# Routing each sequence inside the output projection, into one region per expert, with the modulation weights loaded early and the clearing moved into the attention

## The reference

```
x1  = x0 + gate * (attention(...) @ Wo)
h   = layernorm(x1) * scale + shift
lg  = router(rmsnorm(h))              # [2048 tokens, 8 experts]
top2, weights = top 2 of lg, softmax over the two
xs  = rows of h sorted by expert      # 4096 rows, ragged groups
y   = gelu(xs @ Wg[e]) * (xs @ Wu[e]) @ Wd[e]
x2  = x1 + gate * combine(y, weights)
mod1 = silu(c1) @ L1_wmod             # [4, 3072], six parts of 512, used in layer 1
```

## Time and profile before

| | us |
|---|---|
| median of 3 executions | 2810.01 |
| lowest, highest | 2806.75, 2813.84 |
| the profiled execution, its own time | 2821.85 |
| span of that execution in the trace | 2820.1 |
| mean granted TensorE clock, share of full | 0.934 |
| busy over the span: PE, DVE, ACT, POOL | 2440.6, 1751.6, 1275.8, 1083.1 |

### The profile page before, as it was taken

The page is one execution under the profiler, slowest core; times in us unless marked ns, Lnnn a source line. Parts: engine busy times, 40 slices in busy tenths (PEclk is TensorE's granted clock), DMA queues, the critical chain, the costliest instruction groups (busy, mean ns, idle before and its releaser), DMA issues. The chain is left out here.

```text
span 2820.1 us, 34326 instructions
## 1 busy us (share of the span) xinstructions
PE 2440.6 (87%) x10156; PEld 1660.9 (59%) x10156; DVE 1751.6 (62%) x2565; ACT 1275.8 (45%) x2546; POOL 1083.1 (38%) x1090
## 2 busy tenths in 40 slices
PE   7999959999999986966999994769898757699889
PEld 5778825555555544845888883535445216588767
DVE  4330239999999994644555553679999977211133
ACT  3223038999999982324555552732323113211121
POOL 0102035666666654542000002278898973111110
PEclk9999979999999997967999997889999988899989
DMA  5253343434444427757766765544444435100022
GB/s 176 84 170 129 97 107 106 128 107 124 112 119 117 113 61 226 252 194 256 233 227 227 233 209 160 172 151 153 161 166 156 176 118 173 53 23 22 19 93 67
DMA packets 269652, 399.91 MB, mean 142 GB/s; under 512 B 33392, under 2 KB 116352, under 8 KB 269536
## 3 DMA queue, kind: packets, MB, share of 16 engines
q1 hardware_dynamic: 234848, 347.64, 39.0%
q10 hardware_dynamic: 28704, 33.08, 3.4%
q0 software_dynamic: 5984, 17.73, 1.9%
HBM read 304.09 MB, written 94.31 MB: 141 GB/s over the span
## 5 line engine op out<-in xcount | busy, mean ns | idle before, releaser
L1020 ACT ACTIVATE attn_probs<-attn_ps_score,attn_nmax 128x512 f32<-128x512 f32 x512 | 342.8, 674 | 2.6 <-DVE attn_nmax L1094 2.6
L2480 PE MATMUL scan_ps_o<-scan_qs,scan_sel 128*128 128x512 f32 x512 | 265.3, 635 | 84.3 <-DVE scan_qs L2424 81.7
L2442 DVE TENSOR_TENSOR_SCAN scan_st<-scan_ps_dec,scan_kv 128x512 f32<-128x512 f32 x256 | 305.4, 1207 | 9.9 <-POOL scan_kv L2394 9.8
L928 PE MATMUL attn_ps_score<-attn_KK,attn_X 64*128 64x512 f32 x512 | 215.0, 466 | 20.6 <-ACT attn_probs L1020 20.2
L2480 PEld LDWEIGHTS scan_ps_o<-scan_qs,scan_sel 128*128 128x128 f32 x512 | 88.9, 194 | 232.2 <-DVE scan_qs L2424 153.9
L1108 DVE SCALAR_TENSOR_TENSOR attn_mixed<-attn_probs,attn_cf,attn_mixed 128x512 f32<-128x512 f32 x256 | 193.5, 756 | 9.1
L1083 DVE TENSOR_REDUCE attn_raw<-attn_ps_score 128x2 f32<-128x1024 f32 x128 | 156.4, 1222 | 42.4 <-PE attn_ps_score L928 41.1
L928 PE MATMUL attn_ps_score<-attn_KL,attn_X 64*128 64x512 f32 x512 | 172.9, 422 | 0.0
L85 POOL MEMSET head_ident<- 128x128 f32 x1 | 0.2, 204 | 439.6 <-POOLq L2828 439.6
L2394 POOL TENSOR_TENSOR scan_kv<-scan_vb,gla_gk 128x512 f32<-128x512 f32 x128 | 160.7, 1277 | 12.2 <-DMA scan_vb<-gv 5.4
L928 PE MATMUL attn_ps_score<-attn_KK,attn_Y 64*128 64x512 f32 x512 | 160.1, 397 | 1.3 <-POOL attn_Y L822 1.3
(11 more groups left out here) (438 smaller groups left out, 6803.8 us busy)
## 6 DMA issues: line engine op xcount, KB each, us to landing
scan_vb<-gv SPq DMA_DIRECT2D x256, 256.0 KB
moe_raw<-in_L_ffn_gating SPq DMA_DIRECT2D x92, 512.0 KB
attn_spread<-rows SPq DMA_DIRECT2D x64, 384.0 KB
moe_raw<-in_L_ffn_linear SPq DMA_DIRECT2D x46, 512.0 KB, 5.4
rows_x<-out_zeros SPq DMA_DIRECT2D x23, 512.0 KB, 8.4
moe_xb<-rows_x SPq DMA_DIRECT2D x23, 512.0 KB, 6.1
rows_y<-moe_y ACTq DMA_DIRECT2D x23, 512.0 KB, 6.5
sg<-proj_tile SPq DMA_DIRECT2D x32, 256.0 KB, 2.0
```

The lines of the kernel that those rows point to most:

```text
L928: last = nc.tensor.matmul(ps_score[n][:, j, :], weights, y[p][half, :], start=(r == 0), stop=(r == len(terms) - 1))
L1020: nc.scalar.activation(probs[b][:, at_j, :], ps_score[n][:, j, :], ACT.Exp, bias=nmax[b][:, at_j:at_j + 1], accum_out=Z[b][:, at_j:at_j + ...
L2442: V.tensor_tensor_scan(st[r][:, :], ps_dec[n % 2][:, :], kv[r][:, :], 0.0, ALU.mult, ALU.add).then_inc(st_ready, 1)
L2480: nc.tensor.matmul(ps_o[w][:, :], sel[:, P - GPH - GPH * d:2 * P - GPH - GPH * d], qs[i % RING][:, :], start=(d == 0), stop=(d == HALF - 1 ...
```

## The change

- `rows_x` becomes 8 regions of 2048 rows, one per expert. A token's row in its expert's region needs only the counts of the tokens before it, so each sequence is ranked (`choice`), counted (`count`) and placed (`places`) by itself inside the projection. The logits move from behind a sequence's fourth tile to behind its third, for the sequence before.
- POOL scatters tiles 0 to 11 within the projection, from tile 10 on, and tiles 12 to 15 at the head of the expert mixture. That stage keeps the table of experts and makes a table of each block's first row, which SP reads before it loads a block's rows. Block 0 always belongs to expert 0 and begins at row 0, so neither its weights nor its rows wait for a table.
- The clearing (now 33.5 MB, 32 transfers of 1 MB) is issued in the attention, one behind each unit's `inputs`.
- The six parts of the modulation weights are loaded in the projection; parts 2 to 5 go into buffers that the projection has finished with. Parts 0 and 1 are multiplied behind its last tile and come back to SBUF with eight small transfers in the expert mixture; parts 2 to 5 are multiplied at that stage's start, and POOL bounds the two gates.

```diff
+        zeros = m.sb("zeros", [P, D])
...
+                sp.dma_start(at(fill, u).rearrange("o p t d -> p (o t) d"),
+                             zeros[:, :].unsqueeze(1).to_broadcast([P, E * B * T // (U * P), D])).then_inc(zeroed, 16)
...
+            nc.gpsimd.memset(zeros[:, :], 0.0).then_inc(const_ready, 1)
...
+        late = s["late"] if h is not None else None
+        raw_w = [late[0][:, i, :] if h is not None else m.sb(f"raw_w{i}", [P, D])[:, :] for i in range(RAWS)]
...
-        FILL_FROM = 2
+        SCATTER_BEHIND = 2 * TT + 2
+        MOD_WITH = {3: 2, 6: 0, 9: 1, 13: 3, 14: 4, 15: 5}
...
-                if cleared is not None:
-                    fill = cleared.rearrange("(n p t) d -> n p (t d)", p=P, t=2)
-                    many = fill.shape[0]
-                    if n == FILL_FROM:
-                        sp.wait_ge(zeros_ready, 1)
-                    for k in range((n - FILL_FROM) * many // (NT - FILL_FROM) if n >= FILL_FROM else 0,
-                                   (n + 1 - FILL_FROM) * many // (NT - FILL_FROM) if n >= FILL_FROM else 0):
-                        sp.dma_start(fill[k], zeros[:, :]).then_inc(zeroed, 16)
-            if cleared is not None:
-                sp.wait_ge(zeroed, 16 * many)
...
+                if h is not None and n in MOD_WITH:
+                    k = MOD_WITH[n]
+                    if k == 2:
+                        sp.wait_ge(wlo_ready, KC)
+                    if k == 3:
+                        sp.wait_ge(stored[0], 16 * B // 2)
+                        sp.wait_ge(hn_ready, B - 1)
+                    if k == 4:
+                        sp.wait_ge(tr_done, DC * (B - 1))
+                        sp.wait_ge(scaled, TT * (B - 1))
+                    if k == 5:
+                        sp.wait_ge(olo_ready, NT)
+                    dst = s["mod_x"][:, k, :, :] if k < 2 else late[k - 2][:, :, :]
+                    sp.dma_start(dst, wmod[:, :, k * D:(k + 1) * D]).then_inc(mod_w_in[k], 16)
...
+            def scatter(n):
+                pool.wait_ge(rows_ready, n // TT + 1)
+                pool.wait_ge(shifted, n + 1)
+                scatter_rows(nc, s, n)
...
+                if h is not None:
+                    if n == 1:
+                        route_constants()
+                    if n % TT == 1 and n > TT:
+                        scale(n // TT - 1)
+                    if n >= SCATTER_BEHIND:
+                        scatter(n - SCATTER_BEHIND)
+                for n in range(NT - SCATTER_BEHIND, NT - 2 * TT):
+                    scatter(n)
                 scale(B - 1)
+                for n in range(NT - 2 * TT, NT - TT):
+                    scatter(n)
...
+            def modulation(k):
+
+                pe.wait_ge(mod_w_in[k], 16)
+                pe.wait_ge(gated, NT - 2 + k)
+                for c in range(DC):
+                    last = nc.tensor.matmul(bank[(NT + k) % BANKS][0:B, :], s["sT"][:, 1, c, :], s["mod_x"][:, k, c, :],
+                                            start=(c == 0), stop=(c == DC - 1))
+                last.then_inc(mod_done, 1)
+
+            def count(b):
+
+                if b == 0:
+                    pe.wait_ge(route_const, N_ROUTE)
+                pe.wait_ge(chosen_ready, b + 1)
+                if b == B - 1:
+                    pe.wait_ge(placed, b)
+                flat = s["chosen"][:, TT * b:TT * (b + 1), :].rearrange("p n e -> p (n e)")
+                for k, x in enumerate((earlier, ones)):
+                    last = nc.tensor.matmul(ps_logit[:, (1 + k) * TT * E:(2 + k) * TT * E], x[:, :], flat, start=True, stop=True)
+                last.then_inc(count_done, 1)
...
-                if h is not None and n % TT == TT - 1 and n > TT:
+                if h is not None and n % TT == 2 and n > TT:
                     logits(n // TT - 1)
+                if h is not None and n % TT == 1 and n >= 2 * TT:
+                    count(n // TT - 2)
+            if h is not None:
+                for k in two:
+                    modulation(k)
             turn(B - 1)
             if h is not None:
+                count(B - 2)
                 logits(B - 1)
+                count(B - 1)
...
+                if h is not None and b and t == TT - 1:
+                    router(b - 1)
                 if h is not None and b >= 2 and t == 1:
-                    router(b - 2)
                     squares(b - 2)
             root(B - 1)
             store(B - 1)
+            if h is not None:
+                for k in two:
+                    modulation(k)
+                squares(B - 2)
             take(B - 1)
             if h is not None:
-                for b in (B - 2, B - 1):
-                    router(b)
-                    squares(b)
+                router(B - 1)
+                squares(B - 1)
+                act.wait_ge(mod_stored, 32)
...
+            def choice(b):
...
+                rc.step(V.tensor_tensor(beats[:, :, :, :], pj, pi, ALU.is_gt))
+                rc.link(V.tensor_tensor(ties[:, :, :, :], pj, pi, ALU.is_equal))
+                rc.link(V.tensor_tensor(ties[:, :, :, :], ties[:, :, :, :], below[:, :, :, :], ALU.mult))
+                rc.link(V.tensor_tensor(beats[:, :, :, :], beats[:, :, :, :], ties[:, :, :, :], ALU.add))
+                rc.link(V.tensor_reduce(rank[:, :, :], beats[:, :, :, :], AX.X, ALU.add))
+                V.tensor_scalar(s["chosen"][:, tiles, :], rank[:, :, :], 2.0, None, ALU.is_lt).then_inc(chosen_ready, 1)
+                rc.step(V.tensor_scalar(s["first_e"][:, tiles, :], rank[:, :, :], 0.0, None, ALU.is_equal))
+                rc.link(V.tensor_scalar(s["second_e"][:, tiles, :], rank[:, :, :], 1.0, None, ALU.is_equal))
+
+            def places(b):
+
+                tiles = slice(TT * b, TT * (b + 1))
+                counts = lambda k: ps_logit[:, (1 + k) * TT * E:(2 + k) * TT * E].rearrange("p (n e) -> p n e", e=E)
+                base = s["base"]
+                dve.wait_ge(count_done, b + 1)
+                for t in range(TT):
+                    n = TT * b + t
+                    rc.link(V.tensor_tensor(base[:, n + 1, :], base[:, n, :], counts(1)[:, t, :], ALU.add))
+                V.tensor_tensor(place[:, :, :], base[:, tiles, :], counts(0), ALU.add).then_inc(placed, 1)
+                dve.wait_ge(placed, b + 1)
+                for c, one in enumerate((s["first_e"], s["second_e"])):
+                    rc.link(V.tensor_tensor(pick[:, :, :], place[:, :, :], one[:, tiles, :], ALU.mult))
+                    rc.link(V.tensor_reduce(s["row"][:, c, tiles], pick[:, :, :], AX.X, ALU.add))
+                V.tensor_copy(row_x[:, :, tiles], s["row"][:, :, tiles]).then_inc(rows_ready, 1)
...
+                    if h is not None and b:
+                        choice(b - 1)
                 if t == 2 and b:
                     after(b - 1)
+                if h is not None and t == 1 and b >= 2:
+                    places(b - 2)
+            if h is not None:
+                places(B - 2)
             after(B - 1)
+            if h is not None:
+                choice(B - 1)
+                places(B - 1)
...
-            for k in range(6):
-                sp.dma_start(mod_w[k][:, :, :], wmod[:, :, k * D:(k + 1) * D]).then_inc(mod_in[k], 16)
-            sp.wait_ge(experts_ready, 1)
-            sp.wait_ge(mod_done, 6)
...
-                sp.dma_start(xb[n % 2][:, :, :], xg[n]).then_inc(xb_in[n % 2], 16)
+                r = nc.sync.value_load(start_of[0:1, n:n + 1], min_val=0, max_val=LAST_START) if n else 0
+                sp.dma_start(xb[n % 2][:, :, :], s["rows_x"][bass.ds(r, BLK), :].rearrange("(t p) d -> p t d", p=P)
+                             ).then_inc(xb_in[n % 2], 16)
 
             load_weights(0)
             sp.wait_ge(scattered, 16 * 2 * NT)
             load_rows(0)
+            sp.wait_ge(experts_ready, 2)
             load_rows(1)
             for n in range(NBLK):
                 if n + 1 < NBLK:
                     load_weights(n + 1)
                 if n + 2 < NBLK:
                     load_rows(n + 2)
+                if n == 1:
+                    for q in two:
+                        for c in range(DC):
+                            at = q * D + c * P
+                            sp.dma_start(s["modT1"][:, q, c, :], s["mod"][1, :, at:at + P].rearrange("b p -> p b"),
+                                         allow_slow_non_contiguous=True).then_inc(modT_in, 16)
+            sp.wait_ge(modT_in, 16 * 2 * DC)
...
+            for n in range(NT - TT, NT):
+                scatter_rows(nc, s, n)
...
+            for j, k in enumerate(GATES):
+                line = mod_row[k]
+                pool.wait_ge(mod_taken, k - 1)
+                ch.link(nc.gpsimd.tensor_scalar(sgn, line, 0.0, 2.0, ALU.is_ge, ALU.mult))
...
+            for k in range(2, 6):
+                pe.wait_ge(s["mod_w_in"][k], 16)
+                for c in range(DC):
```

(4 more changed lines are left out.)

278 lines of the change are left out of this document (135 added, 143 removed).

## The result

The kernel after takes 2788.4 us, median of five runs (2783.7 to 2798.5), beside 2808.9 for the kernel before in the same runs (2803.2 to 2813.8): ratio 0.9937, interval 0.9909 to 0.9964, 20.5 us less. Forecast were 2769.0, 40.8 less. Two further sets of the same kernel, measured later, gave 2786.9 (0.9902, 0.987 to 0.9935) and 2780.6 (0.9892, 0.9873 to 0.9911). So the kernel is faster by 20 to 32 us where 41 were forecast; the sign was right and the size too large, by 9 us in the last set and by half the forecast in the first.

A forecast was written before the change was run, and what follows sets the result against it. DVE fills the attention and PE the mixture; between them engines work alone, with a 74.3 us head. Head -54.0, projection +7.0 and tail +6.2 sum to -40.8: from the 2810.0 median to 2769, range 2757 to 2787.

The forecast's parts named there:

- the 8.7 us behind the last scatter issue: Head: landing, loading block 0, turning and splitting it after the last scatter issue, taken as 8.7 us as before.
- the clearing at cost 0: Attention: the clearing moved there is hidden, cost 0, with bounds 0 and 5.1 us a unit.
- POOL in the tail, "to 22": Tail: POOL scales to 12.0 us after the last tile's end, then scatters tiles 8 to 11 (10.1), to 22.
- rival 3: Head: the weights or a later link set gate(0) at 30 rather than 20, giving 2779; chance 0.10.
- `inputs` has been issued when the fill comes: Attention: `inputs` is issued before the fill, and what stands behind is needed most of a unit (21 us) later.
- DVE stays at 97%: Attention: sign of being right, DVE's busy share stays at 97% in the after profile.
- Rival 4: Attention: clearing holds up mask rows or values on an in-order queue; at 5.1 us a unit, 2932; chance 0.04.
- Rival 1: Tail: POOL and DVE in each other's way, issues at 1.9 + 0.3, stage ends 4 to 10 later, 2776; chance 0.20.
- The row that spoke against the page, an issue of 1.89: Profile before: a scatter issue took 1.89 beside DVE's subtractions; the page says tensor_tensor does not stall descriptor generation.
- in DVE's gaps: Projection: choice and places, 5.3 us in a sequence of about 27 us, fit in DVE's gaps.
- The three terms: Projection, before PE's last tile: third logits 3.6, two counts 1.0 together, clock lost after logits 2.4; sum +7.0.
- Rival 2: Tail and head: clock stays up, last logits at 3.6 (-3.4), first gate product's twelve faster (-2.4), 2763; chance 0.17.

The follow-up runs named there:

- three edits together: Kernel after with first expert's down weights behind the first rows, third logits behind the last tile, third sequence's squares behind the last take: 2784.4 us, ratio 0.9888.
- the early choice: Kernel after with each sequence's choice put before the wait for the fourth tile's matmuls instead of behind the norm: 2783.8 us, ratio 0.9889.
- the third profile: The kernel after measured and profiled a third time, nothing changed: 2780.6 us, ratio 0.9892.
- the tail rearranged: Kernel after with earlier choice, third sequence's counts, places and two scatters moved earlier, squares later: 2777.8 us with late down weights, 2779.7 without.

## Why the prediction was right or wrong

**The steps that failed**, in the prediction's own terms: the 8.7 us behind the last scatter issue, whose landing part was 1.75 and became 5.35 (3.6 us); the clearing at cost 0, which was 2.3 to 3.2; and POOL in the tail, "to 22", which was 24.9 and 28.3 with its drain. In the projection a wait of 1.9 us had no term.

**The direction and the mechanism.** The head was the place, and it shrank to 23.6 by what was forecast: eight scatter issues instead of 32 behind the stage's start, 1.28 apart, and the weights asked for at once. The scatters of the projection cost PE nothing in this kernel, as forecast; the experiment with the third logits moved shows that the last tile had no room left, a wait of 1.42 that the third logits cover. The mixture kept PE full.

**The head, -50.1 instead of -54.0.** The failed term is "the 8.7 of before" behind the last issue. In it were 1.75 us for the scatters' landing, and that number came from a trace in which the weights had long landed. After, the last scatters land beside 3 MB of weights, and it is 5.35. The experiment with the down weights moved shows the cause: 3.1, and 3.0 and 2.7 in two further kernels. The rest of the term held (1261.71 to 1268.46 is 6.75, forecast 6.95). The weights' own landing, which I took as the risk and rival 3, was no limit: the last chunk was cast at +16.9, forecast 15, and moving it gained nothing in the end. Rival 3 did not occur: 23.6, not 30.

**The attention, +3.2 instead of 0** (+2.3 over all executions). "`inputs` has been issued when the fill comes" is the failed step: it left out the fill of the unit before, behind which this unit's `attn_Wx` and `attn_spread`, both part of `inputs`, are issued late. I priced the fill by DMA's idle share, 0.42 plus 0.25, where the resource was SP's queue in order: 9.0 us of its spare 12.9 a unit. One fill fits in the queue, and yet `attn_spread` lands late in some units, POOL starts late, and DVE's instructions beside it take 2.3 us more in all. "DVE stays at 97%", which I gave as a sign of being right, could not show this, since the loss is inside DVE's busy time. That the time of SP's queue is what the further fills run out of is shown by its waits going to zero while DMA stays at 0.6. Rival 4 named the queue in order rightly, and its small chance was fair for one fill; but the spare time left, 3.8 us a unit, is less than a further 0.5 MB takes.

**The tail, +7.8 instead of +6.2.** Half of the 1.6 between them is the kernel before's mean; the tail after took 28.4 where 27.6 were forecast. POOL "to 22" is the failed step. I let its scatters begin at the scaling's end, but they need the third sequence's places, which came 2.4 later (1230.86), since its choice took 6 instead of 2.9 beside the scaling. And a stage doesn't end for POOL with its last issue: the drain's record ends 3.1 later. So the stage's end came 1.4 us behind DVE's last instruction (1243.55, the start of the mixture 1244.97), with POOL's drain the last, where I had 5.6 us of slack. With three edits together POOL alone set the end. Rival 1 was half right. POOL and DVE did stand in each other's way, but the scatter issues stretched little (1.20 and 1.45 for the first two, 0.97 to 1.05 for the others); DVE's small operations did, 6.0 in the tail instead of 2.9. The Trainium skill, SBUF — State Buffer, "Who interferes with whom", names both kinds: an instruction with two SBUF inputs (L1551, 2.52 beside POOL and 0.42 without it) and tensor_scalar, which may lock the ports (L1556, 1.25 and 0.17). The experiment with the early choice agrees with it in both rows. The row that spoke against the page, an issue of 1.89, has a weaker like in the tail, the 1.20 and 1.45 beside DVE's additions, 0.7 us in all. What I called "in DVE's gaps" is true of the time, not of the neighbour.

**The projection, +8.2 instead of +7.0.** The three terms were third logits 3.6, counts 1.0, clock 2.4. The counts show 0.5 to 0.6 each in PE's rows, as forecast. Taking the third logits away took 4.0 to 5.2 from the projection, against 3.6 + 2.4 forecast. What was not in the sum is the second and third logits' wait for the places, 1.31 and 0.58 in the third profile; and that wait does not add to the clock's fall, since removing it left the projection where it was. The clock's fall stands behind the pauses for logits and varies from 0 to 3.2 between executions of one kernel, so a term of this kind has no value better than its mean, 1.8 over the eight places in the four executions of the kernel before with and without fills; I took 2.4 from two of them. With these waits, 1.9, and 1.6 for the clock behind the third logits (7.06 to 7.34 for the last tile) the sum is 8.1. That the forecast came within 1.2 of 8.2 is partly luck: its two errors had opposite signs.

**Rival 2**, the clock staying up, did not occur: the last logits took 7.00 and the first gate product starts at 0.78 and 0.63 a product.

**The range.** 2757 to 2787 missed the first set's 2788.4 by 1.4 and held the two later ones. Its upper end doesn't follow from its own terms, 2779 and 4 for the spread being 2783. It was made from unknowns of the projection, tail and head; it had nothing for a small cost in the attention, and too little for the medians, which differ by 8 us between sets of one kernel.

**What stays open.** Of the miss between the spans, 1.6 us are in stretches for which no change was forecast, and may be scatter. The first set's 20.5 us against 25.7 and 31.8 in the later ones have no cause that a run shows. Why SP's issues are held for 3.8 us behind a fill that uses a fraction of the engines is not settled. No version tried is faster than the kernel after beyond the measurement: the best, with the tail rearranged, 2777.8 and 2779.7 beside 2780.6 to 2788.4.

## What to carry to other kernels

A load that is made early to get off the critical path still lands beside something: the time to land of what it now stands beside has to be priced anew, not taken from the trace in which it stood alone. Before putting transfers on an in-order queue under a busy stage, read that queue's own waits, not the DMA engines' share; here 64 us in 100 of waits took one fill of 1 MB a unit and not one and a half. And an engine that stays full can still lose time: compare its busy us for the same instructions, not its share. And where a stage ends with a barrier, POOL, which issued the indirect transfers here, ended some 3 us after its last one.
